# Expert layers run once per pair of samples instead of once per sample, with 23 sorted blocks instead of two times 15

## The reference

```python
# layer 3: 8 experts, top 2, D=128, H=512
probs = softmax(x @ Wr.T); topv, topi = top_k(probs, 2)
for e: h = gelu(x @ W1[e] + b1[e]); y = h @ W2[e] + b2[e]; out += combine[e] * y
# layer 7: 8 experts, top 2, weights divided by their sum
probs = softmax(x @ Wg);   topv, topi = top_k(probs, 2); topv /= topv.sum()
for e: h = silu(x @ w_gate[e] + b_gate[e]) * (x @ w_up[e] + b_up[e])
       y = h @ w_down[e] + b_down[e];        out += combine[e] * y
```

## Time and profile before

| | before |
|---|---|
| median of three runs | 1499.15 us (1498.88 to 1500.82) |
| the profiled execution | 1508.51 us |
| its span, from the first to the last instruction | 1506.4 us |
| PE busy | 1151.1 us, 76% |
| DVE busy | 920.1 us, 61% |
| ACT busy | 662.9 us, 44% |
| POOL busy | 280.6 us, 19% |
| expert weights loaded | 60 x 836 KB and 60 x 578 KB |
| mean granted share of the TensorE clock | 0.886 |

### The profile page before, as it was taken

One profiled execution on the slowest core, in us unless ns is written; L12 is line 12 of the kernel. 1 busy time (PEld: TensorE's weight loads), 2 busy tenths in 40 slices (PEclk: granted clock), 3 DMA queues, 4 the chain that ended last, 5 costly groups with the idle time before them and its releaser, 6 DMA issues.

```text
span 1506.4 us, 16451 instructions
## 1 busy us (share of the span) xinstructions
PE 1151.1 (76%) x5428; PEld 761.0 (51%) x5428; DVE 920.1 (61%) x2079; ACT 662.9 (44%) x1289; POOL 280.6 (19%) x261
## 2 busy tenths in 40 slices
PE   0988656667869989976897767755867999978774
PEld 0534522233757446666775423433635745547674
DVE  4575679998627384234484778987786355334432
ACT  1532267524634343452452476436943434443321
POOL 1200112425140201203202211213242020020222
PEclk9998767877989998989999868986988999988987
DMA  8000000003564000536540000003513600033763
GB/s 330 0 1 0 1 0 0 0 1 103 188 200 125 20 1 4 172 101 212 172 166 28 7 0 0 0 1 104 172 43 104 200 15 1 0 131 121 271 205 131
DMA packets 57641, 125.50 MB, mean 83 GB/s; under 512 B 5320, under 2 KB 38224, under 8 KB 57168
## 3 DMA queue, kind: packets, MB, share of 16 engines
q1 hardware_dynamic: 52880, 111.14, 22.5%
q0 software_dynamic: 4096, 8.40, 1.7%
q10 hardware_dynamic: 576, 4.87, 0.8%
HBM read 109.31 MB, written 15.07 MB: 83 GB/s over the span
## 4 chain that ended last, share of the span: by engine, by line
PE 46%; DVE 18%; ACT 13%; issue 9%; DMA 8%; POOL 5%; SPq 1%; DVEq 0%; another core or an unknown queue 0%; POOLq 0%; ACTq 0%
PE ps L1739 6%; PE ps L1801 5%; PE ps L1529 5%; DMA expert_ring<-in_e_dram 4%; PE ps L1477 4%; PE ps L1642 3%; PE ps L1712 3%; DVE up L1230 3%; PE ps L1771 2%; POOL slots_dram L639 2%; POOL up L646 2%; PE ps L1582 2%; PE ps L1839 1%; ACT big L862 1%; PE ps L1790 1%
## 5 line engine op out<-in xcount | busy, mean ns | idle before, releaser
L1739 PE MATMUL ps<-big,expert_ring 128*128 128x128 f32 x1440 | 200.1, 289 | 45.6 <-DMA expert_ring<-in_e_dram 18.1
L1739 PEld LDWEIGHTS ps<-big,expert_ring 128*128 128x128 f32 x1440 | 184.6, 201 | 66.7 <-issue 34.5
L587 POOL TENSOR_TENSOR rstd<-ve,nhalf 128x4 f32<-128x4 f32 x44 | 48.2, 1096 | 692.3 <-DVE ve L1024 548.0
L1230 DVE TENSOR_TENSOR_SCAN up<-cv,big 128x512 f32<-128x512 f32 x128 | 151.5, 1223 | 24.7 <-ACT cv L821 18.1
L1642 PE MATMUL ps<-big,consts 128*128 128x512 f32 x256 | 149.1, 713 | 2.2 <-DVE big L1237 2.2
L1712 PE MATMUL ps<-expert_ring,big 128*128 128x128 f32 x960 | 130.0, 279 | 11.5 <-DVE big L1350 6.4
L624 POOL TENSOR_TENSOR big<-big,mt 128x512 f32<-128x512 f32 x64 | 85.1, 1333 | 263.2 <-ACT mt L814 133.6
L1712 PEld LDWEIGHTS ps<-expert_ring,big 128*128 128x128 f32 x960 | 119.3, 194 | 18.4 <-DVE big L1350 7.1
L1659 PE MATMUL ps<-q,row_pick 96*128 96x512 bf16 x128 | 54.5, 441 | 89.3 <-DVE big L1237 57.4
L1801 PE MATMUL ps<-big,weights 128*128 128x512 f32 x256 | 116.1, 598 | 0.8 <-DVE big L1402 0.8
L859 ACT ACTIVATE key<-ps,expert_ring 128x128 f32<-128x128 f32 x240 | 68.6, 369 | 106.2 <-PE ps L1739 94.6
(11 more groups left out here) (249 smaller groups left out, 1990.7 us busy)
## 6 DMA issues: line engine op xcount, KB each, us to landing
expert_ring<-in_e_dram SPq DMA_DIRECT2D x60, 836.0 KB
expert_ring<-in_e_dram SPq DMA_DIRECT2D x60, 578.0 KB
big<-slots_dram SPq DMA_DIRECT2D x24, 256.0 KB, 3.2
results_dram<-mt SPq DMA_DIRECT2D x24, 256.0 KB, 4.5
weights<-in_w_dram ACTq DMA_DIRECT2D x1, 3072.0 KB, 14.8
slots_dram<-big SPq DMA_DIRECT2D x2, 960.0 KB, 16.0
weights<-in_w_dram SPq DMA_DIRECT2D x1, 1600.0 KB, 13.4
big<-slots_dram SPq DMA_DIRECT2D x8, 192.0 KB, 3.8
```

The source lines that it names most:

```text
L1230: dve.tensor_tensor_scan(UP[s][:, j, PAD:PAD + T], CV[s][:, j, :], BIG2[s][:, j, :], 0.0, ALU.mult, ALU.add).then_inc(m_scan[s], 1)
L1739: last = pe.matmul(bank4(s, r if m else b % 2)[:, k, :], ring[:, q % RING, r * T + k * P:r * T + (k + 1) * P], XGT[s][:, b // 4, b % 4 * P ...
```

## The change

One pass of an expert layer now takes both samples of a stream. Their 1024 tokens make 2048 pairs, which are sorted into `NBLK = 2 * 2 * T // P + NE - 1` = 23 blocks. Two passes of 15 become one of 23, in both streams and in both expert layers: 92 blocks where there were 120.

For that both samples of a stream have to stand in front of the expert layer together. `PLAY` gives the order: layers 0 to 2 for the first sample and for the second, layer 3 for both, layers 4 to 6 for the first and for the second, layer 7 for both. The buffers of a stream are still there once, so `after_previous` makes the layer norm of each layer wait for the end of what stands before it in `PLAY`; after an expert layer that is the end of both samples.

In an expert layer there are now 16 scatters and 16 gathers, two turns and two sets of logits, one chain of `route` over eight chunks, and six groups of sorted rows instead of four, the last two of which take the place of groups 0 and 1 (`GROUPS_AT`). The softmax is no longer on the way to the positions: the top two are taken from the logits, and the exponentials are made beside the scatter. The gathered rows of the second sample lie in MT. Two more 450 KB parts of the DRAM scratch are zeroed at the start. The table `RUNS` is new for every engine.

```diff
-NBLK = 2 * T // P + NE - 1
+PAIR = 2
+NBLK = PAIR * 2 * T // P + NE - 1
+NGRP = (NBLK + 3) // 4
...
+GROUPS_AT = {1: (2, 3), 5: (4,), 10: (5,)}
+
+
+PLAY = [(0, 0), (1, 0), (2, 0), (0, 1), (1, 1), (2, 1), (3, 0),
+        (4, 0), (5, 0), (6, 0), (4, 1), (5, 1), (6, 1), (7, 0)]
...
 RUNS = {
     "pe": [
-        1, 1, 1, 1, 1, 1, 8, 1, 4, 5, 2, 2, 2, 2, 2, 2, 5, 4, 2, 2, 2, 2, 1, 1, 2, 6, 30, 1, 10, 2, 1, 9, 1,
...
-        1, 1, 5, 1, 19, 49],
+        1, 2, 1, 1, 1, 2, 8, 1, 4, 5, 2, 2, 1, 1, 1, 1, 2, 2, 2, 2, 1, 2, 2, 5, 4, 2, 3, 5, 40, 2, 1, 23, 1,
...
+        1, 1, 4, 1, 30, 1, 1, 8, 1, 1, 1, 5, 2, 6, 1, 8, 1, 1, 1, 2, 1, 9, 1, 1, 2, 1, 1, 3, 1, 29, 75],
...
         def whole(programs, s):
 
-            for i in range(s, NB, NS):
-                for program in programs:
-                    yield from program(i)
+            for layer, r in PLAY:
+                if layer in programs:
+                    yield from programs[layer](r * NS + s)
...
+                    for h in range(PAIR):
+                        for r in range(2):
+                            for c in range(NC):
+                                j = r * C2 + h * NC + c
+                                yield
+                                if h == r == c == 0:
+                                    pool.wait_ge(g.pos[s], g.pos.at(s, 0))
+                                    pool.wait_ge(zeroed, 64)
+                                pool.indirect_dma_start(xs_d[s], bass.IndirectOffsetOnAxis(ap=posu[s][:, j:j + 1], axis=0),
+                                                        xh[h][:, c, :], None).then_inc(scattered[s], 16)
+                    for h in range(PAIR):
+                        for r in range(2):
+                            for c in range(NC):
+                                j = r * C2 + h * NC + c
+                                yield
+                                if h == r == c == 0:
+                                    for half in range(2):
+                                        pool.wait_ge(ys_out[s][half], 16 * (NGRP // 2) * (m + 1))
+                                pool.indirect_dma_start(YG[s][h][:, r, c * P:(c + 1) * P], None, ys_d[s],
+                                                        bass.IndirectOffsetOnAxis(ap=posu[s][:, j:j + 1], axis=0))\
+                                    .then_inc(gathered[s][h][r], 16)
...
+            def after_previous(layer, s):
+                at = PLAY.index((layer, s // NS))
+                if at and not in_general[0]:
+                    before, r = PLAY[at - 1]
+                    dve.wait_ge(x_done[before][s], x_done[before].at(r * NS + s % NS, -1))
...
             def experts(m, name):
                 def layer(s):
                     g = moe[m]
-                    yield from turn(g.n, s)
-                    yield from route(m, name, s)
+                    for h in range(PAIR):
+                        yield from turn(g.n, s, h)
+                        logits(m, name, s, h)
+                    yield from route(m, s)
                     for k in range(2):
                         yield from turn_slots(g, s, k)
                     for b in range(NBLK):
-                        if b == 1:
-                            for k in range(2, 4):
-                                yield from turn_slots(g, s, k)
+                        for k in GROUPS_AT.get(b, ()):
+                            yield from turn_slots(g, s, k)
```

More of the change, by code:

```diff
@@ L155, in at @@
     def at(self, i, k):
-        return self.a_round(i // NS) + self.base + (self.total if k == -1 else k + 1)
+        return self.before(i // NS) + self.base + (self.total if k == -1 else k + 1)
 def turns(who):
@@ L164, in expert_loads @@
 def expert_loads():
[L166 to L167 removed]
+    labels = [[None] + [(m, k, label) for m in range(2) for label in SP_MOE + ["out"] * (PAIR * m)]
+              for k in range(NS)]
     met = [0] * NS
@@ L251, in network, with early @@
[L251 to L255 removed]
+        def early(s, at, n, rows=P):
+            return KEY[s][0:rows, at:at + n]
@@ L299, in S, with before, __init__ @@
             nth[engine] = n + 1
-            base = raised.get((engine, n), 0)
-            raised[engine, n] = base + total
-            return Signal([stage_sems[engine, n, s] for s in range(NS)], base, total,
-                          lambda r: (r - general_round[0]) * raised[engine, n])
+            layer = now[0]
+            raised[engine, n, layer] = total
+            def before(r):
+                if in_general[0]:
+                    return 0
+                return sum(raised.get((engine, n, l), 0) for l, _ in PLAY[:PLAY.index((layer, r))])
+            return Signal([stage_sems[engine, n, s] for s in range(NS)], 0, total, before)
         class Norm:
-            def __init__(self, turned=True):
+            def __init__(self, turned=True, samples=1):
                 self.var = S("dve", 1)
                 self.rs = S("pool", 1)
-                self.done = S("dve", 1)
+                self.done = S("dve", samples)
                 if turned:
-                    self.T = S("pe", 1)
-                    self.xT = S("act", 1)
+                    self.T = S("pe", samples)
+                    self.xT = S("act", samples)
         layer_begins()
@@ L826, in route, with per @@
                 act.wait_ge(g.sh[s], g.sh.at(s, 0))
-                act.activation(lg[s][:, 1], lg[s][:, 0], ACT.Exp).then_inc(g.ex[s], 1)
+                act.activation(shifted[s], shifted[s], ACT.Exp).then_inc(g.ex[s], 1)
+            def per(g):
+                return 2 if g is moe[1] else 1
             def slots_turned(g, s, k):
@@ L841, in layer @@
                     yield from turned(g.n, s)
+                    yield from turned(g.n, s, k=1, read=g.lg)
                     yield from route(g, s)
@@ L1039, in layer_norm, with pair_norm @@
             def layer_norm(layer, s):
                 yield
-                if layer:
-                    dve.wait_ge(x_done[layer - 1][s], x_done[layer - 1].at(s, 0))
-                else:
+                if not layer:
                     dve.wait_ge(x_in[s], 16)
-                yield from norm(norms[layer], s, X, XH)
+                after_previous(layer, s)
+                yield from norm(norms[layer], s, (X[s], XH[s]))
+            def pair_norm(layer, s):
+                yield
+                after_previous(layer, s)
+                yield from norm(norms[layer], s, (X[s], XH[s]), (X[s + NS], XH2[s]))
@@ new lines, in route @@
+                step(dve.tensor_reduce(used, cnt4[s], AX.X, ALU.add))
+                step(dve.tensor_tensor_scan(ends, ones[:, 0:1].broadcast_to([P, NE]), used, 0.0, ALU.mult, ALU.add))
+                dve.tensor_tensor(past[s], ends[0:1].unsqueeze(1).broadcast_to([1, NBLK, NE]),
+                                  cn("blocks", 1)[:, 0:NBLK].unsqueeze(2).broadcast_to([1, NBLK, NE]), ALU.is_le)
+                step(dve.tensor_tensor(first, ends, used, ALU.subtract))
+                dve.tensor_reduce(whof[s][:, 0:NBLK], past[s], AX.X, ALU.add)
```

363 lines of the change are left out of this document (179 added, 184 removed), and 58 rows, old and new, of the table RUNS.

## The result

The changed kernel takes 1421.0 us, median of four runs (1419.5 to 1423.3), the kernel before beside it 1499.0 (1498.2 to 1500.8). The ratio is 0.948, 95% interval 0.946 to 0.950: 78 us less. I had forecast 1409 us with a range of 1378 to 1450. The profiled execution took 1419.5 us; its span is 1417.7, forecast 1416.7.

The account below looks back on a forecast made before the run. The bound: how well two streams cover each other's waits in a fixed order. Distances between turns along stream 0, then stream 1's tail, summed to a 1416.7 us span; + 2.1 and - 9.4 to the median gave 1409 us, range 1378 to 1450.

Parts of the forecast that it names:

- start of L0s2: End of layer 2 of sample 0, where layer 0 of sample 2 begins: order the same, at 335.3 us.
- L0s2: Layer 0 of sample 2 beside the second half of layer 2 of sample 1: 108 us.
- L1 and L2 of sample 2: Layers 1 and 2 of sample 2 beside layers 0 and 1 of sample 3, same neighbours: 173.5 us.
- handover: From stream 1's turn of layer 3 to stream 0's turn of layer 4, POOL's queue the path: 63.9 us.
- L5 and L6 of sample 0: Layers 5 and 6 of sample 0, with stream 1's gathers beside them and PE free: 109 us.
- L4s2: Layer 4 of sample 2, beside layers 4 to 6 of the other stream: 55 us.
- L5 and L6 of sample 2: Layers 5 and 6 of sample 2, with two full neighbours: 115 us.
- first sorted rows: From stream 1's turn of layer 7 to its first sorted rows on PE, with eleven blocks: 50.2 us.
- 23 blocks: Stream 1 alone at the end: 61.4 us for 15 blocks before, + 8 x 3.92 and 0.9: 93.7 us.
- rival of the fast tail: Last stretch at PE's pace, 2.7 us a block instead of 3.92: 1373 us; chance 0.14 for below 1385.
- rival of the uncovered bubble: Expert-layer handovers between streams, and layer 0 of sample 2, not covered: up to 1461 us; chance 0.23 for 1435 to 1495.
- slower than before: Layers 4 to 6 of both streams beside each other: 20% longer the gain is gone, 25% gives 1535; chance 0.04.

Follow-up runs that it names:

- the old order with moved stores: Kernel before, with the store of sample 2's output behind the last weight load of sample 3's layer 7 instead of its eighth: 1506.6 us, ratio 0.997.
- the corner with 120 blocks: Changed kernel with seven further blocks that hold no pair, 30 blocks a stream and expert layer: 1525.0 us, ratio 1.021 to the kernel before.
- doubled blocks: Changed kernel, in seven of 23 blocks weights loaded into two slots and every matmul done from both: 1610.8 us, ratio 1.077 to the kernel before.

## Why the prediction was right, and where it was not

**The sum.** The span came out within 1 us, partly because errors of both signs cancel. By its steps, measured less forecast: start of L0s2 -9.9 us, L0s2 +7.1, L1 and L2 of sample 2 +7.3, layer 3 of stream 0 -4.4, handover +1.0, L4s0 +1.0, L5 and L6 of sample 0 +14.5, L4s2 -10.5, L5 and L6 of sample 2 +7.8, layer 7 of stream 0 +3.9, L6s3 -0.5, first sorted rows -3.7, 23 blocks -13.0, end +0.3.

The first of them I had taken as "the order is the same", and it is not: L1s1 now stands ahead of L2s0, and the tables of layer 0 are new. The gain lies in layer 0: the turn of L1s0 is at 162.2 us before and 152.5 after, and from there to L0s2 both take 173 us. Which entry of the tables does it was not tried. The zeroing that I put at nothing did cost nothing at the first turn (36.8 us before, 36.5 after); the two further stores move 0.9 MB, not 3.

**L5 and L6 of sample 0** are the term most off: 109 us taken, 123.5 measured. I gave this pair less than the second one because stream 1's gathers stood beside it; it cost the same as the second (122.8). Layer 4 of sample 2 I priced near the mean of 40.5 and 65.8, and it was at the low end, 44.5. Which neighbour makes the difference was not tried.

**The last stretch.** I took 3.92 us a block; by the same kind of window it is 3.44. The window of the earlier trace rows holds a stop that the changed kernel's trace does not have. Timelines of ScalarE and PE before:

```profile
1443.60 1.14 ACT L859 ACTIVATE key<-ps,expert_ring 128x128 f32<-128x128 f32 x4 [5.56 <-remote]
```

```profile
1440.33 1.06 PE L1712 MATMUL ps<-expert_ring,big 128*128 128x128 f32 x8
1444.89 1.13 PE L1739 MATMUL ps<-big,expert_ring 128*128 128x128 f32 x8 [3.51 <-issue]
```

PE lost 3.5 us there, 0.2 us for each of 15 blocks, about half of the difference. Another 0.16 us is PE's busy time of a block, 3.22 us at a granted clock of 0.88 and 3.06 at 0.96. The rival of the fast tail, 2.7 us a block, did not come: waits for loads go on to the last blocks. It took half of the bytes to reach that pace, and then only in the last twelve.

**From the span to the median** I took 9.4 us off, the distance of before's profiled execution from its median. In the changed kernel that distance is -1.5 us. This one step is 11 of the 12 us by which 1409 missed 1421. The sum was built from the rows of an execution with stops: behind the start-up, the profile of before has six of over 5 us (the longest 14.1), each beside indirect DMAs on POOL, and the changed kernel's has none. Five of the six stand at the same place in the trace of the old order with moved stores, which ran on the first chip. One of these on ScalarE, first the kernel before, then that run:

```profile
429.45 0.60 ACT L833 ACTIVATE big<-ps 128x512 f32<-128x512 f32 x1 [12.08 <-issue]
```

```profile
427.27 0.60 ACT L833 ACTIVATE big<-ps 128x512 f32<-128x512 f32 x1 [11.84 <-issue]
```

That chip has 1510.0 us for the kernel before, near the 1508.5 of the profiled execution. That the stops made the 9.4 us is argued from this, not shown.

**The handover.** 63.9 us forecast, 64.9 measured, and the reason I gave was only one of two. I put it down to POOL's queue ahead of stream 0's gathers, and taking eight of these off the way changed nothing. PE comes to the turn last, by 2 to 4 us, from stream 1: its routing, its 16 scatters, its first rows at 783.4, and its eight blocks. POOL is on this way too, by the scatters. The rival of the uncovered bubble named the right place, but most of PE's standing there was already in my sum, and its further 15 us did not come. I also expected two runs of 32 indirect DMAs on POOL. Only layer 3 has one; in layer 7 the scatters end at 1293.7 and the gathers start at 1316.5.

**The blocks.** I priced the 28 blocks at 94 us "if each of them stood on the path alone" and laid the new turns out afresh rather than take 94 off. The number does not tell the two ways apart: 1499 - 94 = 1405 would have been about as near. That would have been luck, because the two halves of the change are not worth 78 us as a sum: in the old order the removed blocks are worth 30 us, the new order with all 120 is a loss of 32. This I did not see. The rival "slower than before" had this mechanism, streams that no longer cover each other, and it is real in the corner with 120 blocks; the 28 blocks less outweigh it because in the new order next to nothing hides a block.

## What to carry to other kernels

Price removed work in the schedule in which it will be missing, not in the one in which it stands: the same block cost 1.1 us in one order and 3.8 in the other, and its matmuls are equal in both. When a change removes work and reorders the rest, run the two corners between before and after; here each half alone would have given the wrong picture. Ahead of carrying over the distance between a profiled execution and the median, see whether the trace has stops that nothing in it explains.

## What the runs showed of the hardware

- With indirect DMAs being issued on POOL, ScalarE, VectorE and PE can stand still for 5 to 19 us (once for 21.9, of which 15 beside them) with no releaser in the trace. All four traces of one chip have such stops, and so has the first profile of the kernel before (its chip is not on record). Of the eight traces of two other chips seven have none over 5 us behind the start-up, and the eighth only PE's waits ahead of doubled blocks; the kernel before took 1510 us on the chip with stops and 1493 to 1499 on the others. What holds the engines was not found.
- A ring of four slots gives a block each 3.5 us at 270 GB/s with 836 KB loads over the whole stretch, and each 3.1 us at 304 GB/s in its last twelve blocks; with 418 KB loads these come at PE's own 2.7 us. With two slots taken by one block the same ring falls behind by up to 5.7 us at a time between 1400 and 1580 us.
- The same 575 matmuls took PE 71.95 us of busy time where it waited for loads (granted clock 0.96) and 66.46 where it hardly did (1.00). The clock is only a part of this: some 290 of them took 34.83 and 32.40 us with 1.00 in both.
